# Moving the squares and their sums of two LayerNorms from VectorE to ScalarE in a fused vision and text kernel

## What is computed

```python
h = tok(x, ...)                         # 16 images, 64 channels, 128 x 128: 1024 tokens of 64 each,
                                        # by offsets, bilinear sampling at 8 points, attention over them
h = concatenate([h, txt], axis=1)       # 1024 + 128 tokens
h = h + scan(_layernorm(h), ...)        # first LayerNorm; a step by 128-wide states
h = h + moe(_layernorm(h), ...)         # second LayerNorm; 16 experts of width 128, top 2 of them weighted

def _layernorm(x, axis=-1, eps=1e-05):
    m = jnp.mean(x, axis=axis, keepdims=True)
    v = jnp.var(x, axis=axis, keepdims=True)
    return (x - m) / jnp.sqrt(v + eps)
```

## Time and profile before

| | |
|---|---|
| Time of three runs | 2227.41 us median (2227.31 to 2228.99) |
| The profiled execution | 2234.98 us, of which its span 2233.2 us |
| Busy in the span | PE 2042.9 (91%), DVE 1842.9 (83%), ACT 1121.3 (50%), POOL 1453.0 (65%) |

### The profile page before, as it was taken

One profiled execution on the slowest core, in us unless ns is written; L12 is line 12 of the kernel. 1 busy time (PEld: TensorE's weight loads), 2 busy tenths in 40 slices (PEclk: granted clock), 3 DMA queues, 4 the chain that ended last, 5 costly groups with the idle time before them and its releaser, 6 DMA issues.

```text
span 2233.2 us, 42161 instructions
## 1 busy us (share of the span) xinstructions
PE 2042.9 (91%) x13857; PEld 1544.3 (69%) x13857; DVE 1842.9 (83%) x4580; ACT 1121.3 (50%) x2472; POOL 1453.0 (65%) x1657
## 2 busy tenths in 40 slices
PE   2468899999999999999999999999999999999989
PEld 1356677767677777767677776767777676777655
DVE  1336898989889898989989898998988899898886
ACT  1225455555555555555555555555545555544443
POOL 0378888577675758767575776857576785758600
PEclk9768999999999999999999999999999999999999
DMA  8787656366663647666464666646466665522200
GB/s 194 212 237 190 188 143 198 96 188 190 168 175 115 193 122 202 179 174 192 119 186 110 196 176 174 197 132 177 112 187 171 181 195 145 165 81 79 59 3 6
DMA packets 363271, 346.58 MB, mean 155 GB/s; under 512 B 49456, under 2 KB 313776, under 8 KB 362928
## 3 DMA queue, kind: packets, MB, share of 16 engines
q1 hardware_dynamic: 313904, 209.60, 34.8%
q0 software_dynamic: 49152, 134.28, 20.3%
HBM read 205.90 MB, written 137.89 MB: 154 GB/s over the span
## 4 chain that ended last, share of the span: by engine, by line
PE 78%; DVE 12%; issue 7%; ACT 2%; DMA 1%; POOL 1%; DVEq 0%; POOLq 0%; SPq 0%; ACTq 0%
PE bank_h L650 12%; PE bank_o L659 12%; PE bank_h L651 10%; PE bank_d L750 10%; PE bank_d L740 10%; PE bank_z L669 5%; PE bank_p L686 4%; PE bank_a L762 4%; DVE hid L1025 2%; PE bank_p L705 2%; DVE v_sb L1160 2%; DVE v_sb L1153 2%; PE bank_a L775 2%; PE bank_p L704 1%; PE bank_p L710 1%
## 5 line engine op out<-in xcount | busy, mean ns | idle before, releaser
L596 POOL DMA_INDIRECT gath<-table,idx x1024 | 1122.1, 1096 | 278.3 <-issue 238.6
L650 PE MATMUL bank_h<-xsplit,w 128*128 128x384 f32 x1536 | 589.6, 384 | 13.4 <-DVE hid L1025 12.4
L651 PE MATMUL bank_h<-xsplit,w 128*128 128x384 f32 x1536 | 521.0, 339 | 0.0
L834 ACT ACTIVATE silu<-bank_h 128x384 f32<-128x384 f32 x768 | 382.3, 498 | 262.1 <-PE bank_h L651 250.4
L1025 DVE TENSOR_TENSOR hid<-silu,bank_h 128x384 f32<-128x384 f32 x768 | 415.9, 549 | 58.1 <-ACT silu L834 51.7
L650 PEld LDWEIGHTS bank_h<-xsplit,w 128*128 128x128 f32 x1536 | 293.0, 191 | 113.0 <-issue 66.5
L1125 DVE TENSOR_TENSOR wsam<-gath,cw 128x1024 f32<-128x1024 f32 x256 | 312.9, 1222 | 43.9 <-PE bank_d L740 23.5
L659 PE MATMUL bank_o<-hid,w_sb 128*64 128x384 f32 x1536 | 335.2, 515 | 14.5 <-DVE scaled L1032 13.2
L616 POOL TENSOR_TENSOR lns<-lns,neghalf 128x3 f32<-128x3 f32 x96 | 88.7, 924 | 336.9 <-DVE lns L1004 335.5
L651 PEld LDWEIGHTS bank_h<-xsplit,w 128*128 128x128 f32 x1536 | 293.9, 191 | 3.2
L740 PE MATMUL bank_d<-eye,wsam 128*128 128x128 f32 x2048 | 278.1, 280 | 15.3 <-DVE wsam L1125 13.6
(11 more groups left out here) (157 smaller groups left out, 2559.8 us busy)
## 6 DMA issues: line engine op xcount, KB each, us to landing
table<-pixmaj SPq DMA_DIRECT2D x80, 1024.0 KB, 10.3
xin<-x_dram SPq DMA_DIRECT2D x256, 256.0 KB
table<-pixmaj SPq DMA_DIRECT2D x32, 960.0 KB
table<-pixmaj SPq DMA_DIRECT2D x16, 1088.0 KB
gath<-table,idx POOLq DMA_INDIRECT x1024
out_dram<-ob SPq DMA_DIRECT2D x48, 96.0 KB, 6.7
gath<-w_dram SPq DMA_DIRECT2D x4, 512.0 KB, 9.0
interp_sb<-interp_dram SPq DMA_DIRECT2D x1, 1024.0 KB, 5.0
```

The costliest lines, as they stand in the source:

```text
L596: pool.indirect_dma_start(out=gath[buf][:, p, :, :].rearrange("p a c -> p (a c)"), out_offset=None, in_=table[par], in_offset=bass.Indirec ...
L650: mm(bank[:, 0:GC], w12[:, e, which, 0, :], xsplit[gp][:], start=True, stop=False)
L651: mm(bank[:, 0:GC], w12[:, e, which, 1, :], xsplit[gp][:], start=False, stop=True).then_inc(ready, 1)
L834: nc.scalar.activation(silu[e % 2][:], bank_h[r][:, 0:GC], ACT.Silu).then_inc(silu_done, 1)
```

## The change

In both LayerNorms the square, its sum and the scaling leave VectorE. ScalarE gets one instruction for each of the 3 tiles of a group: the function Square on 128x64 elements, with the accumulating output that leaves the sum over the 64 in `lns`. GpSimd gets the multiplication by 1/64 and the addition of epsilon, directly ahead of its power. Two semaphores are added: `ln_mid` tells ScalarE that `lnx` is there, `ln_sq` tells GpSimd that the sums are there. The pieces P1 and P5 thus appear on ScalarE's list too, and all five `ORDER` strings are new (one line of PE's in the steady part is shown of each; then the edits in GpSimd's, ScalarE's and VectorE's programs).

```diff
-        "mJmJIaaJxaJKIJzaIJaaJJaaIBJDJDDIDlDJKDJIDlDJItmuJmJvlJIJlamJIJmxJKIlJzIlJamJBmJIDaJDlDJIDalDJaDmJDKD",
...
+        "mJamJaIJxaJKIJzaIJaaJJaaIBJDJDIlDJKDJIDlDJmDJIDmtJluJIvJlJImJKmxJIlJzaJlIJmaBJmIDaJDlDIDJaDlJDamDJKD",
...
                         n = 2 * NGRP * b + 2 * args[0] + (1 if kind == "P1" else 2)
+                        pool.wait_ge(ln_sq, n)
+                        nc.gpsimd.tensor_scalar(lns[:, 1, :], lns[:, 0, :], 1.0 / C, EPS, ALU.mult,
+                                                ALU.add).then_inc(ln_var, 1)
                         pool.wait_ge(ln_var, n)
                         nc.gpsimd.tensor_tensor(lns[:, 2, :], lns[:, 1, :], neghalf[:, 0:GT],
                                                 ALU.pow).then_inc(ln_rstd, 1)
...
+                    elif kind in ("P1", "P5"):
+                        n = 2 * NGRP * b + 2 * args[0] + (0 if kind == "P1" else 1)
+                        act.wait_ge(ln_mid, n + 1)
+                        wait(act, ln_rstd, n)
+                        for k in range(GT):
+                            last = nc.scalar.activation(lnsq[:, k, :], lnx[:, k, :], ACT.Square,
+                                                        accum_out=lns[:, 0, k:k + 1])
+                        last.then_inc(ln_sq, 1)
...
-                link(ln, tt(lnx[:], src, spread(lns[:, 0, :], 2, C), ALU.add))
-                link(ln, tt(lnsq[:], lnx[:], lnx[:], ALU.mult))
-                link(ln, red(lns[:, 0, :], lnsq[:], AX_X, ALU.add))
-                ts(lns[:, 1, :], lns[:, 0, :], 1.0 / C, EPS, ALU.mult, ALU.add).then_inc(ln_var, 1)
+                tt(lnx[:], src, spread(lns[:, 0, :], 2, C), ALU.add).then_inc(ln_mid, 1)
```

More of the change, by code:

```diff
@@ L127 @@
     ("O", "sp"): [(i,) for i in range(3)],
+    ("P1", "act"): [(i,) for i in range(3)],
     ("P1", "dve"): [(i,) for i in range(3)],
@@ L137 @@
     ("P4", "dve"): [(i,) for i in range(3)],
+    ("P5", "act"): [(i,) for i in range(3)],
     ("P5", "dve"): [(i,) for i in range(3)],
@@ L177 @@
[L177 to L181, removed]
@@ L192 @@
[L192 to L195, removed]
+        "aaaaaaaaaaaaaaaabbbbbbbbcdehiaaaaaaalalmmlaaalammllmamalaabbbbbbbblcmdmellmhmilaltmumvalaaalxamzJmaJ",
@@ new lines @@
+        "lJaBaDJIDJaDJlDImDJImDJalDJIDJKaJalamJmIlJJtIulvJmJImlxIzJKJaJBalDbJImDJImDJblDJIDJbDbJlDJmDImtJlubb",
+        "bvJKIlbJmcJmdexlzIJlJImBJmDJlDIDJDDJKDIlDJmDJItmulJvhJiIJlJImamaJxaJKIJzaIJaJaJaaIBJDJDIDlDJKDJIDlDJ",
+        "mDJItmuJlvJIJlJImJxmJKIlJzaJlIJmaBJmIDaJDlDIDJaDlJDamDJKDItmJuaJlIaJlvIJamJbmbJIbbbJbxbJKIblJzIlJcmJ",
+        "BmJIDdDJlDJIDeDlDJmDJKDItmJuJlIJlvhJiImJamJaIJxaJKIJzaIJaaJJaaIBJDJDIDlDJKDJIDlDJIDmtJmuJlvJIJlIJmJx",
+        "mJKIlJzaJlIJmaBJmIDaJDlJDIDalDJaDmJDKDItmJuaJlIaJlvIJamJbmbJIbbbJbxbJKIblJzIlJcmJBmJIDdDJlDJIDeDlDJm",
@@ new lines @@
+        "mbJIbbbJbxbJKIblJzIlJcmJBmJIDdDJlDJIDeDlDJKDmDJItmJuJlIJlvhJiImJamJaIJxaJKIJzaIJaJaJaaIBJDJDIlDJKDJI",
+        "DlDJIDmDJmtJluJIvJlJImJKmxJIlJzaJlIJmaBJmIDaJDlDJIDalDJaDmJDKDItmJuaJlIaJlvIJamJbmbJIbbJbbxbJKIblJzI",
+        "lJcmJBmJIDdDJlDJIDeDlDJKDmDJItmJuJlIJlvhJiImJamJaIJxaJKIJzaIJaaJJaaIBJDJDIlDJKDJIDlDJmDJIDmtJluJIvJl",
+        "JImJKmxJIlJzaJlIJmaBJmIDaJDlDJIDalDJaDmJDKDItmJuaJlIaJlvIJamJbmbJIbbbJbxbJKIblJzIlJcmJBmJIDdDJlDJIDe",
+        "DlDJmDJKDItmJuJlIJvlhJIimJImJaJxaJaKIJzIaJaJaJaIaBJDJDIDlDJKDJIDlDJmDJItmuJlvJIJlJImJxmJKIlJzaJlIJma",
@@ new lines @@
+        "BJmIDaJDlDJIDalDJaDmJDKDItmJuaJlIaJlvIJamJbmbJIbbbJbxbJKIblJzIlJcmJBmJIDdDJlDJIDeDlDJmDJKDItmJuJlIJl",
+        "vhJiImJamJaIJxaJKIJzaIJaaJJaaIBJDJDIlDJKDJIDlDJmDJIDmtJluJvIJlJImJKmxJIlJzaJlIJmaBJmIDaJDlIDJaDlJDam",
+        "DJKDIDmtJauJlIaJlvIJamJbmbJIbbbJbxbJKIblJzIlJcmJBmJIDdDJlDJIDeDlDJmDJKDItmJuJlIJlvhJiImJamJaIJxaJKIJ",
+        "zaIJaJaJaaIBJDJDIlDJKDJIDlDJmDJIDmtJluJIvJlJImJKmxJIlJzaJlIJmaBJmIDaJDlDIDJaDlJDamDJKDItmJuaJlIaJlvI",
+        "JamJbmbJIbbbJbxbJKIblJzIlJcmJBmJIDdDJlDJIDeDlDJKDmDJItmJuJlIJlvhJiImJamJaIJxaJKIJzaIJaJaJaaIBJDJDIDl",
@@ new lines @@
+        "DJKDJIDlDJmDJItmuJlvJIJlJImJKmxJIlJzaJlIJmaBJmIDaJDlDJIDalDJaDmJDKDItmJuaJlIaJlvIJamJbmbJIbbbJbxbJKI",
+        "blJzIlJcmJBmJIDdDJlDJIDeDlDJmDJKDItmJuJlIJlvhJiImJamJaIJxaJKIJzaIJaJaJaaIBJDJDIDlDJKDJIDlDJmDJItmuJl",
+        "vJIJlJImJKmxJIlJzaJlIJmaBJmIDaJDlDJIDalDJaDmJDKDItmJuaJlIaJlvIJamJbmbJIbbbJbxbJKIblJzIlJcmJBmJIDdDJl",
+        "DJIDeDlDJKDmDJItmJuJlIJlvhJiImJamJaIJxaJKIJzaIJaaJJaaIBJDJDIlDJKDJIDlDJmDJIDmtJluJIvJlJImJKmxJIlJzaJ",
+        "lIJmaBJmIDaJDlDIDJaDlJDamDJKDItmJuaJlIaJlvIJamJbmbJIbbbJbxbJKIblJzIlJcmJBmJIDdDJlDJIDeDlDJmDJKDItmJu",
@@ new lines @@
+        "JEDJaJalamJsmJJtulJwmJmxJzJaJBaslDJmDJmDJDJDJDJlDJmDmtJuEJwlbJmcJmdxJzlJmBJsmDJDDJDDJDlDJmDJgtmuJhJw",
+        "JlJmamaJxaJEJaJaJzaJaaBJDsJDDDJDJDlDJmDJtmuJJJwlJmJxmJJaJzlJmaBJmDsaDJDDJaDlJDamDJDtmJuaJEaJlJamwJmJ",
+        "JxJbJzlJcmJBmJDsdDJDJDDlDJmDJDtmJguJJlhJwmJamJaJxaJEJaJaazJJaaBJDsJDDDJDJDlDJDmtJmuJJwJlJmJxmJJaJzlJ",
+        "maBJmsDaJDJDDalDJaDmJDDtmJuaJEaJlJamwJmJJxJbJzlJcmJBmJDsdDJDJDDlDJmDJDtmJguJJlhJwmJamJaJxaJaEJaJaJza",
+        "JaBJDsJDDJDJDlDJmDJDmtJuJJwlJmJmxJJaJzlJmaBJmDsaDJDDJaDlJDamDJDtmJuaJEaJlJamwJmJJxJbJzlJcmJBmJDsdDJD",
@@ new lines @@
+        "JDDlDJmDJDtmJguJJlhJwmJamJaJxaJEJaJaazJJaaBJDsJDDJDJDlDJmDJDmtJuJJwlJmJmxJJaJzlJmaBJmDsaDJDDJaDlJDam",
+        "DJDtmJuaJEaJlJamwJmJJxJbJzlJcmJBmJDsdDJDJDDlDJmDJDtmJguJJlhJwmJamJaJxaJEJaJaazJJaaBJDsJDDJDJDlDJmDJD",
+        "mtJuJJwlJmJmxJJaJzlJmaBJmDaJDsDJDalDJaDmJDDtmJuaJEaJlJamwJmJJxJbJzlJcmJBmJDsdDJDJDDlDJDmDJtgmJuJJlhJ",
+        "wmJamJaJxaJEJaJaJzaJaaBJDsJDDJDJDlDJDmDJmtJuJJwlJmJmxJJaJzlJmaBJmDaJDsDJDalDJaDmJDDtmJuaJEaJlJamwJmJ",
+        "JxJbJzlJcmJBmJDsdDJDJDDlDJDmDJtgmJuJJlhJwmJamJaJxaJEJaJaazJJaaBJDsJDDJDJDlDJmDJDmtJuJJwlJmJmxJJaJzlJ",
@@ new lines @@
+        "maBJmDaJDsDJDalDJaDmJDDtmJuaJEaJlJamwJmJJxJbJzlJcmJBmJDsdDJDJDDlDJmDJDtgmJuJJlhJwmJmJaJxaJaEJaJaJzaJ",
+        "aaBJDsJDDDJDJDlDJmDJtmuJJJwlJmJxmJJaJzlJmaBJmsDaJDDJDalDJaDmJDDtmJuaJEaJlJamwJmJJxJbJzlJcmJBmJDsDJdD",
+        "JDDlDJmDJDgtmJuJJlhJwmJamJaJxaJEJaJaazJJaaBJDsJDDJDJDlDJmDJDmtJuJJwlJmJmxJJaJzlJmaBJmDsaDJDJaDlJDamD",
+        "JDDmtJauJEaJlJamwJmJJxJbJzlJcmJBmJDsdDJDJDDlDJmDJDtmJguJJlhJwmJamJaJxaJEJaJaJzaJaaBJDsJDDJDJDlDJmDJD",
+        "mtJuJJwlJmJmxJJaJzlJmaBJmDsaDJDDJaDlJDamDJDtmJuaJEaJlJamwJmJJxJbJzlJcmJBmJDsdDJDJDDlDJDmDJtmJguJJlhJ",
@@ new lines @@
+        "wmJamJaJxaJEJaJaJzaJaaBJDsJDDDJDJDlDJmDJtmuJJJwlJmJmxJJaJzlJmaBJmDaJDsDJDalDJaDmJDDtmJuaJEaJlJamwJmJ",
+        "JxJbJzlJcmJBmJDsdDJDJDDlDJmDJDtmJguJJlhJwmJamJaJxaJEJaJaJzaJaaBJDsJDDDJDJDlDJmDJtmuJJJwlJmJmxJJaJzlJ",
+        "maBJmDaJDsDJDalDJaDmJDDtmJuaJEaJlJamwJmJJxJbJzlJcmJBmJDsdDJDJDDlDJDmDJtgmJuJJlhJwmJamJaJxaJEJaJaazJJ",
+        "aaBJDsJDDJDJDlDJmDJDmtJuJJwlJmJmxJJaJzlJmaBJmDsaDJDDJaDlJDamDJDtmJuaJEaJlJamwJmJJxJbJzlJcmJBmJDsdDJD",
+        "JDDlDJmDJDtmJguJJlhJwmJmJJxJEJJJzJBJDsJDDJDJDlDJmDJDmtJuJJwlJmJmxJJJzlJmJBmDJsDJDlDJmDJDDmDJtJEuJlJm",
@@ L448, in build @@
         ln_v = sem("ln_v")
+        ln_mid = sem("ln_mid")
+        ln_sq = sem("ln_sq")
         ln_var = sem("ln_var")
@@ L1223 @@
 SOFT_N = 7
-LN_N = 5
+LN_N = 2
 TOP_N = 12
```

117 lines of the change are left out of this document (43 added, 74 removed).

## The result

| | before | changed |
|---|---|---|
| Median, same chip | 2228.2 us (2227.31 to 2230.71, 4 runs) | 2207.18 us (2204.58 to 2209.07, 4 runs) |
| Ratio | | 0.9898, 95% interval 0.9881 to 0.9915 |
| Span of the profiled execution | 2233.2 us | 2203.9 us |

A forecast was written before the change was run, and what follows sets the result against it. PE was taken to set the pace for most of a period, VectorE in the cluster. Gains 9.2 + 7.9 + 2 = 19 us, less 4 for squares, gave -15: 2227.41 to 2212 us, 8-in-10 range 2198 to 2236.

The forecast's parts named there:

- the cluster: Softmax, gate and weights (S2, P7, S3, P8) on VectorE, once a period: claimed to stay 12 us long and VectorE-bound.
- rival "no change": At the cluster: VectorE cannot follow PE's 0.77 us, saved waits come back elsewhere; 2227 us, chance 0.16.
- The relief itself at nothing: VectorE's LayerNorm work, 1.02 us each, 98 us over 96: costed at nothing since PE's work hides it.
- Outside the steady part I take 2: Outside the 12 periods: two `aa` and two `DD` pairs fewer, at most 2.9 us, taken as 2.
- 12 x 0.77 = 9.2: PE ahead of P6: one `aa` pair a period gone, each saving a 0.77 us wait for `bank_a`; 9.2 us.
- 12 x 0.66 = 7.9: PE behind P9: the `DD` pair gone from every period, each saving a 0.66 us wait for `wide`; 7.9 us.
- the five pairs inside the cluster: Five other pairs fewer between P7 and P9, where PE has time to lose: nothing; 3.8 us at full price.
- 1 in 30 of 115 us: ScalarE's queue: 288 squares, 1.2 us per LayerNorm, 115 us in all, of which 4 us come through.
- The slower rival: ScalarE's queue: squares hold the Silu, `hid` is late; 0.4 us at each of 96 places, 2246 us, chance 0.18.
- few us: Sign of failure on VectorE: its waits for GpSimd's statistics growing by more than a few us.
- "nothing" for GpSimd: GpSimd's 96 scalings, 2.8 us a period against 19 us of waiting for variances: no cost.
- the 10 named: Sign of failure on PE: its waits for `hid` growing by over 10 us.

The follow-up runs named there:

- the pair of experiments: Kernel before with 25 PE piece pairs taken apart: 2229.5 us, ratio 1.0005; the same with square, sum and scaling also left out: 2210.89 us, ratio 0.9912.
- the slow one with the old order: New LayerNorm split in the old order, squares put behind the following Silu on ScalarE, against the kernel before: 2294.5 us, ratio 1.0294.
- the new order alone: New order of all engines with squares, sums and scaling back on VectorE, against the kernel before: 2236.93 us, ratio 1.0044.

## Why the prediction was right, and where it was not

The direction, the range and the size (2212 forecast, 2207 measured, the range 2198 to 2236) held. That it came within 5 us is partly luck: the mechanism (pairs taken apart pay once VectorE has room) was right, but four terms of the sum were off and their errors partly cancelled, as is summed below.

**What bounds the kernel.** Right as a state, incomplete as a rule. Up to the cluster PE was the bound by 0.30 us only. The kernel is balanced: PE waits for ScalarE's single-buffer copies, and as soon as these waits shrink, the same time appears as waits for VectorE. The prediction said this of the cluster ("it would not fit into the old 0.30: that is where the relief is needed"), and the pair of experiments shows it: 0 without relief, 11 us with it. The rival "no change" describes the kernel with the pairs apart and no relief: the pair's time came back as waits for VectorE.

**"The relief itself at nothing".** Wrong by 8.5 us. That was its worth alone in the old order; the profiled executions differ by 5.7 us in the 12 periods and by 5.5 in the last part. In the new order it was worth five times as much, 42 us by the ratios. "Outside the steady part I take 2" held as far as it can be read: the gain is 22.7 us by the ratio, and 20.3 of it lie in the 12 periods. The 13.5 us by which the last part shrank are for a good part work that the new order has moved ahead of the cut.

**"12 x 0.77 = 9.2" and "12 x 0.66 = 7.9".** The second was right to the tenth in waits, once VectorE had room. The first was too large for what it named: with one expert between them, the second A1 of each of the 12 pairs waited 0.44 us in place of 0.77, and 3.9 us were won, not 9.2. In the changed strings they stand further apart, and the waits fell to 16 and 12.3 us, as forecast; this took in the five pairs inside the cluster "counted as nothing". From the old order with relief and pairs apart (0.9912) to the new order without squares (0.9857) are another 12 us, 14.5 by the periods, which no term of the sum had. The list of waits doesn't show them: 9.1 us fewer for `pixmaj` stand against 9.5 more for `hid`, `scaled` and `dispr`. Between these two kernels PE's idle time in the periods fell by 6 us (46.0 to 39.9) and its busy time, for the same products, by 8 (1486.4 to 1478.0). How much of this is those pairs and how much other moves of the strings was not separated, and why the same products took less busy time stays open.

**"1 in 30 of 115 us", 4 us on ScalarE.** The squares were cheaper than taken (0.82 us against 1.2, near the lower bound of 0.77) and more of them came through: 9 us of 96 x 0.82 = 79, 1 in 9. The term was 5 us too small.

**The slower rival.** Its engine and queue were right, the thing behind the squares mostly not. The waits of `hid` for the Silu are 41.3 us in the changed kernel and 38.3 in the slow one with the old order: the Silu isn't what separates them. The copies of `wide` and `v_sb`, from a buffer that PE must have back, are. Only of the small price in the changed kernel does the Silu's path hold a part, at most 2.0 of 8.2 us. The rival put 0.4 us a place on its case and 0.20 on the turning point; measured are 0.1 where the squares stand and 0.6 more one position earlier, enough to turn 21 us of gain into 9 of loss. The Trainium skill, page "ScalarE: Activation LUTs", section "Rules for kernel authors", would leave multiplications on VectorE; the factor that it gives there is for bf16, this work is f32. The traces agree that they are dearer on ScalarE (0.82 us against 0.71), but not that they belong there: in this kernel 98 us taken from VectorE made room that 9 us of ScalarE's time paid for.

**GpSimd and latency.** The scaling took 408 ns in the mean (0.46 taken), 0.20 in the median. At the first place shown, the power ended 2.1 us behind `lnx`, not 2.9, since the scaling took 0.19 there and the squares 0.82. Elsewhere it was late: VectorE waited 9.0 us (9 times) and 2.4 us (4 times) for GpSimd's statistics in 420 to 1967 us. That is over the "few us" named as a sign of failure, and the forecast held all the same: of these 11.4 us PE lost some 1.0, at P6, against the kernel without squares. As a sign it was badly chosen. But "nothing" for GpSimd, and the loads behind its waiting scaling that "did no harm", are too strong: the chain now runs through them for 10% of the span, so by the profile GpSimd has no slack at those places. PE's waits for `hid` grew by 6.9, under the 10 named.

**Summed again with measured sizes.** Relief -8.5; pairs apart, given relief, -11; the rest of the new order -12; squares on ScalarE +9: -22.5, against -22.7 by the ratio. The four are the steps from one kernel to the next, so they close by construction; that isn't a check, and other steps give other sizes (the new order alone +10, relief in it -42, squares +9). The forecast's -19 + 4 came near it because a term that was missing (12) and one set to nothing (8.5) made up for one that was too large (17 for 11) and one too small (4 for 9).

## What to carry to other kernels

- When two engines are within a fraction of a microsecond of each other, price a pair of edits together: here reordering gave 0, relief 8.5 us, and both 19.6. A wait that disappears for one releaser has to be looked for under the next.
- Work moved onto an idle engine costs by its place in that engine's queue. Look for the copy out of a buffer that the busy engine must have back, and put new work behind it: one position was worth 0.6 us at each place here, with a work of 0.82 us.
- Read the waits of the busiest engine for signs of failure. Waits of another engine have to be followed to it: 11 us of VectorE's, for GpSimd, came to 1 us of PE's. Where two kernels share PE's program, the start of each product compared in both traces shows the places that lose the time.

## What the runs showed of the hardware

ScalarE's accumulating output is a second instruction, ACTIVATION_READ_ACCUMULATOR, 191 ns in the mean, that overlaps with the squares on both sides: a square of 128x64 (250 ns) with its sum repeats every 0.25 us (1081.66, 1081.91, 1082.15). I had expected one instruction, and 0.4 us each. GpSimd's scaling of 128x3 took 408 ns in the mean, but 0.19 us at the place shown; the power behind it went from 924 to 1015 ns in the mean. Their medians are 0.20 and 0.88 us (0.88 before too), so the means rest on some long ones, up to 2.3 and 1.9 us. Why these are long was not tried.
